# GpSimd loads the FFN weights, ScalarE takes signs, copies and seven normalizations, VectorE merges statistics and shares the last low parts

## What is computed

```
x = x + dwconv7x7(layernorm_c(x), w_sym)
t = tokens(x)                              # (16, 1024, 192)
h = layernorm(t) @ sign(W1 - mean_g(W1)).T + b1      # 768 hidden, weights in 5 groups of rows
h = gelu(clip(h * 128 / (max|h| + 1e-5)))  # the maximum over a group of 3 images
y = h @ sign(W2 - mean_g(W2)).T + b2
out = t + clip(y * 128 / (max|y| + 1e-5))  # again a group maximum
```

## Time and profile before

| | us |
|---|---|
| median of 3 runs (lowest, highest) | 699.06 (697.81, 699.81) |
| the profiled execution | 697.41 |
| its span, first to last instruction | 695.6 |
| busy: TensorE, VectorE, ScalarE, GpSimd | 510.0, 455.9, 383.2, 217.0 |
| mean granted TensorE clock | 0.884 of full |

### The profile page before, as it was taken

One profiled execution on the slowest core, in us unless ns is written; L12 is line 12 of the kernel. 1 busy time (PEld: TensorE's weight loads), 2 busy tenths in 40 slices (PEclk: granted clock), 3 DMA queues, 4 the chain that ended last, 5 costly groups with the idle time before them and its releaser, 6 DMA issues.

```text
span 695.6 us, 9929 instructions
## 1 busy us (share of the span) xinstructions
PE 510.0 (73%) x3552; PEld 356.9 (51%) x3552; DVE 455.9 (66%) x1106; ACT 383.2 (55%) x612; POOL 217.0 (31%) x195
## 2 busy tenths in 40 slices
PE   4254179995299874656778979997999799778763
PEld 4254179995299873323334535554555455345342
DVE  8988922221068587599888686788878878644432
ACT  3799710000000301443799989997999799787400
POOL 4000100000000000000056756475656557678900
PEclk9778589998599995788999999999999999989865
DMA  8997136654254519900011000131222333142444
GB/s 221 304 333 186 53 82 172 167 167 138 87 149 130 152 49 362 340 0 0 13 55 47 24 24 0 47 91 64 74 69 91 96 109 92 47 135 73 135 138 155
DMA packets 55270, 81.29 MB, mean 117 GB/s; under 512 B 7161, under 2 KB 38905, under 8 KB 55222
## 3 DMA queue, kind: packets, MB, share of 16 engines
q1 hardware_dynamic: 40416, 68.93, 32.2%
q10 hardware_dynamic: 14806, 11.73, 5.7%
HBM read 53.12 MB, written 27.53 MB: 116 GB/s over the span
## 4 chain that ended last, share of the span: by engine, by line
PE 37%; ACT 22%; DVE 17%; DMA 10%; issue 5%; POOL 3%; ACTq 3%; SPq 2%; POOLq 0%; DVEq 0%
PE bank L873 15%; ACT arena L486 9%; ACT arena L480 6%; PE bank L947 5%; DMA arena<-kz_d 5%; DMA arena<-x 4%; DVE am L745 4%; POOL arena L373 3%; DVE arena L726 2%; PE bank L922 2%; DVE arena L672 2%; PE bank L924 2%; ACT arena L504 2%; PE bank L923 2%; ACT arena L466 2%
## 5 line engine op out<-in xcount | busy, mean ns | idle before, releaser
L373 POOL TENSOR_TENSOR arena<-arena 128x512 f16<-128x512 f32 x180 | 204.2, 1174 | 297.3 <-DVE arena L741 297.3
L873 PE MATMUL bank<-arena 128*128 128x112 f32 (+1 forms) x1152 | 137.1, 283 | 45.1 <-DMA arena<-kz_d 29.2
L873 PEld LDWEIGHTS bank<-arena 128*128 128x128 f32 x1152 | 135.5, 199 | 46.7 <-issue 27.0
L480 ACT ACTIVATE arena<-bank,b1s 128x512 f32<-128x512 f32 x180 | 126.1, 703 | 57.4 <-PE bank L924 57.0
L947 PE MATMUL bank<-arena 128*128 128x512 f16 x360 | 110.0, 402 | 30.4 <-ACT arena L504 19.0
L486 ACT ACTIVATE arena<-arena,gm 128x1024 f32<-128x1024 f32 x90 | 102.6, 1161 | 5.6 <-DVE gm L767 5.6
L656 DVE TENSOR_TENSOR arena<-bank,arena 128x512 f32<-128x512 f32 x48 | 33.2, 691 | 103.7 <-PE bank L873 103.6
L745 DVE TENSOR_REDUCE am<-arena 128x1 f32<-128x3072 f32 x30 | 100.3, 3343 | 0.0
L922 PE MATMUL bank<-arena 128*128 128x512 f16 x180 | 71.2, 396 | 33.9 <-DVE arena L734 14.5
L429 ACT ACTIVATE arena<-arena,wmean 51x576 f16<-51x576 f32 (+1 forms) x10 | 7.6, 840 | 136.1 <-DVE wmean L625 136.1
L947 PEld LDWEIGHTS bank<-arena 128*128 128x128 f16 x360 | 34.0, 101 | 79.3 <-issue 35.2
(11 more groups left out here) (115 smaller groups left out, 655.2 us busy)
## 6 DMA issues: line engine op xcount, KB each, us to landing
arena<-park_d SPq DMA_DIRECT2D x44, 384.0 KB, 3.4
arena<-kz_d SPq DMA_DIRECT2D x100, 112.0 KB, 2.8
arena<-kz_d ACTq DMA_DIRECT2D x92, 112.0 KB, 3.2
park_d<-arena SPq DMA_DIRECT2D x6, 1536.0 KB, 13.9
arena<-x SPq DMA_DIRECT2D x8, 1024.0 KB, 8.6
out<-arena SPq DMA_DIRECT2D x32, 256.0 KB, 2.0
kz_d<-arena SPq DMA_DIRECT2D x8, 672.0 KB, 11.3
arena<-x SPq DMA_DIRECT2D x16, 256.0 KB, 9.8
```

The lines of the kernel that those rows point to most:

```text
L373: last = pool.tensor_tensor(out=low_half(u, m, m + 1), in0=yslot(u)[:, 2 * m:2 * m + 2, :], in1=hib(u, m, m + 1), op=ALU.subtract)
L480: act.activation(yslot(s)[:, 2 * m:2 * m + 2, :], m1p[c % 2][:, :].rearrange("p (h n) -> p h n", h=2), ACT.Identity, bias=b1s[:, m:m + 1], ...
L873: last = t.matmul(ps[:, :, lo:hi], WB[BUFS[g]][:, 1 - db, c, :], xn[:, :, lo + db:hi + db], start=(db == 0), stop=(db == -1))
```

## The change

- The ten loads of W1 and W2 are issued by GpSimd, after group 24; it also clears the ends of the transposed weights. Its first memset is cut into six.
- ScalarE makes one sign operation after each band load from group 38 on, and copies the transposed signs out of PSUM (four for W1 behind the band loads, six for W2 first thing in step -2). The sums move to groups 28 to 32, the means' matmul to after group 33.
- Front: for the last unit ScalarE copies before it takes the root of the unit before, and VectorE takes the factors of the unit before in the middle of the last statistics.
- The statistics of channels 0 to 127 are ready by group 45 and are merged for all images at once in group 46; the merging per batch has nine operations and one; four batches instead of five.
- ScalarE does `normal` for half images 1 to 7. In step -2 it takes the root before it copies image 16.
- High parts: ScalarE tiles 0 and 1, VectorE 2 to 5; for half images from 23 on ScalarE 0 to 3 and VectorE 4 and 5. Low parts from half image 23 on: GpSimd tiles 0 to 2, VectorE 3 to 5. TensorE takes the products of the tiles in the order 2 to 5, 0, 1 (from 23 on 3 to 5, 0 to 2).
- `result` of channels 0 to 127 is taken at the end of the step of its products, up to step 29.
- The x of half images 25 to 29 is loaded at step 30 into five buffers; 25 and 26 are transposed in step 31 and 27 in step 39, into PSUM banks that are free by then; 28 and 29 after the final sums of 24 and 25. ScalarE's queue stores their upper channels.

```diff
-BATCH = ((0, 2), (2, 6), (6, 10), (10, 12), (12, 15))
-BSTEP = (-2, -1, 0, 1, 2)
-FREED = {3: 2, 4: 3, 5: 3, 6: 4, 7: 5, 8: 5}
+BATCH = ((0, 2), (2, 6), (6, 10), (10, 15))
+BSTEP = (-2, -1, 0, 1)
...
+ANORM = range(1, 8)
...
+HA, HL, LP = 2, 4, 3
+LAST = FT - LAGH
+ORDER = {False: (*range(HA, MT), *range(HA)), True: (*range(LP, MT), *range(LP))}
...
+def ha(u):
+    return HL if u >= LAST else HA
...
+early = list(range(FT - GT + 1, FT))
+at = XB + WW + WTN
+XE = [*XL, *(view(at + i * RB * C, RB * C).rearrange("p (n c) -> p n c", n=RB) for i in range(2))]
+turned = {v: pair for v, pair in zip(early, ((bank[0], bank[1]), (tA, tB), (m2a, m2b), (xA, xB), (bank[0], bank[1])))}
...
+        if s == FT:
+            sp.wait_ge(tnv, FT)
+            for i, h in enumerate(early):
+                if i == 3:
+                    sp.wait_ge(trQ, FT)
+                sp.dma_start(XE[i].rearrange("p n c -> p (n c)"), park_d[h - 2 * KEPT]).then_inc(ld_g[i], 16)
...
+    for i in range(6):
+        last = pool.memset(view(R + i * WW // 3, WW // 3), 0.0)
+    last.then_inc(blank, 1)
...
+    pool.wait_ge(conv, ROOM[FOURTH] + 1)
+    for q in range(GROUPS):
+        pool.dma_start(w1w[0:RP1, q, :], w1[q * 3 * RP1:(q + 1) * 3 * RP1, :]
+                       .rearrange("(p r) c -> p (r c)", r=3)).then_inc(ld_w, 16)
+        pool.dma_start(w2w[0:RP2, q, :], w2[q * RP2:(q + 1) * RP2, :]).then_inc(ld_w, 16)
...
+    for u in range(LAST):
+        pool.wait_ge(hiV, u + 1)
+        low(u, HA, MT)
+        pool.wait_ge(hiA, u + 1)
+        low(u, 0, HA)
+    for u in range(LAST, FT):
+        pool.wait_ge(hiA, u + 1)
+        low(u, 0, LP)
...
+        if k == PAIRS - 1:
+            bring(k)
         if k:
             deviation(k - 1)
-        if k < PAIRS:
+        if k < PAIRS - 1:
...
+        if g >= 38:
             act.wait_ge(prep_mean, 2)
-            for q in range(GROUPS):
-                sign(w1s[q][0:RP1], w1w[0:RP1, q, :].rearrange("p (r c) -> p r c", r=3), wmean[0:RP1, q:q + 1])
-        if g == 40:
-            for q in range(GROUPS):
-                sign(w2s[q][0:RP2], w2w[0:RP2, q, :].rearrange("p (m f) -> p m f", m=MT),
-                     wmean[0:RP2, GROUPS + q:GROUPS + q + 1])
+            signs(g - 38)
...
+    act.wait_ge(prep_t, 1)
+    for dst, src, ch in ((W1A, t1a, slice(0, P)), (W1Q, t1b, slice(0, P)), (W1M, t1a, slice(0, C1)),
+                         (W1M, t1b, slice(C1, P))):
+        o = dst[ch, 0:n].rearrange("p (g q r) -> p g r q", g=GROUPS, r=3)
+        i = src[ch, :].rearrange("p (g r q) -> p g r q", g=GROUPS, r=3)[:, :, :, 0:RP1]
+        act.activation(o, i, ACT.Copy).then_inc(prep_done, 1)
...
+    def second_weights():
+        act.wait_ge(prep_t, 2)
+        for m in range(MT):
+            act.activation(W2T[:, m, 0:GROUPS * RP2].rearrange("p (g q) -> p g q", g=GROUPS), t2[m], ACT.Copy) \
+                .then_inc(prep_done, 1)
+    def normal(h):
+        act.wait_ge(nm, PAIRS + taken(h // 2))
+        if h >= 2:
+            act.wait_ge(trQ, h - 1)
+        for jj in range(RB):
+            n = RB * h + jj
+            last = act.activation(TN[:, h % 2, jj, :], X1[:, n, :], ACT.Identity, bias=SM[:, n:n + 1], scale=VR[:, n:n + 1])
+        last.then_inc(tnv, 1)
...
+            second_weights()
+            deviation2(0)
             x_alone(0)
             x_alone(1)
-        if s == -2:
-            deviation2(0)
...
-        if 0 <= w < FT:
+        if s > FT and 0 <= w < FT:
             result(w, 0)
...
+            if m < 2 and 0 <= k < FT and 2 * m < ha(k):
+                high(k, 2 * m, 2 * m + 2)
             if m == 0 and 0 <= w < FT:
                 result(w, 1)
+            if m == MT - 1 and 0 <= s - LAG2 and s < FT:
+                result(s - LAG2, 0)
...
+        if s + 2 in ANORM:
+            normal(s + 2)
+    for u in early:
+        act.wait_ge(fin, u + 1)
+        store_upper(act, u, u % Y2R, st_o[u % Y2R])
...
+            if k == PAIRS - 1 and j == NB // 2:
+                factors1(k - 1)
...
+        if 0 < k < PAIRS - 1:
+            factors1(k - 1)
             normal1(k - 1)
         if k < PAIRS:
             stats1(k)
+        if k == PAIRS - 1:
+            normal1(k - 1)
...
+    def lower_whole():
+        dve.wait_ge(bnA, NN)
+        v.tensor_tensor(out=SA[:, :, 0], in0=SA[:, :, 1], in1=SA[:, :, 4], op=ALU.add).then_inc(mixA, 1)
+        v.tensor_tensor(out=SA[:, :, 3], in0=SA[:, :, 1], in1=SA[:, :, 4], op=ALU.subtract).then_inc(mixA, 1)
...
-        if 32 <= g < 48:
-            lower_statistics((g - 32) * per, (g - 31) * per)
-        if 27 <= g < 27 + GROUPS:
-            weight_sums(g - 27)
-        if g == 37:
+        if 32 <= g < 32 + PARTS:
+            lower_statistics((g - 32) * NN // PARTS, (g - 31) * NN // PARTS)
+        if 28 <= g < 28 + GROUPS:
+            weight_sums(g - 28)
+        if g == 35:
             weight_means()
-        if g == 45:
-            weight_copies(0)
+        if g == 32 + PARTS:
+            lower_whole()
...
+        v.scalar_tensor_tensor(out=SM[:, cols], in0=SM[:, cols], scalar=-1.0 / 6.0, in1=VR[:, cols], op0=ALU.mult,
+                               op1=ALU.mult).then_inc(nm, 1)
...
+        v.tensor_copy(hib(u, ha(u), MT), yslot(u)[:, 2 * ha(u):2 * MT, :]).then_inc(hiV, 1)
+        if u >= LAST:
+            dve.wait_ge(hiV, u + 1)
+            low(u, HL, MT)
+            dve.wait_ge(hiA, u + 1)
+            low(u, LP, HL)
+    def low(u, m0, m1):
+        v.tensor_tensor(out=low_half(u, m0, m1), in0=yslot(u)[:, 2 * m0:2 * m1, :], in1=hib(u, m0, m1),
+                        op=ALU.subtract).then_inc(lo2v, 1)
...
-        if -1 <= s <= 5:
-            normal(s + 2)
...
+        order = ORDER[u >= LAST]
+        m = order[i]
+        if i == 0:
+            if u < LAST:
+                pe.wait_ge(lo2, lows(u) - 1)
             if u >= 1:
                 pe.wait_ge(ev2, 2 * u - 1)
+        if u >= LAST and m >= LP:
+            pe.wait_ge(lo2v, 2 * (u - LAST) + (1 if m >= HL else 2))
+        if m == 0:
+            pe.wait_ge(lo2, lows(u))
...
+        if s == FT + 1:
+            pe.wait_ge(ev1, MT * FT)
+            pe.wait_ge(ld_g[0], 16)
+            x_back(early[0], XE[0], xpl)
+            pe.wait_ge(tlo, 2 * FT)
+            pe.wait_ge(ld_g[1], 16)
+            x_back(early[1], XE[1], xpl)
+        if s == FT + LAGF - GT:
+            pe.wait_ge(ev2, 2 * FT)
+            pe.wait_ge(ld_g[2], 16)
+            x_back(early[2], XE[2], xpl)
+    for i in (3, 4):
+        pe.wait_ge(fin, early[i] - 3)
+        pe.wait_ge(ld_g[i], 16)
+        x_back(early[i], XE[i], xpl)
```

156 lines of the change are left out of this document (72 added, 84 removed).

## The result

The changed kernel takes 638.7 us at the median (635.5 to 640.3), the kernel before 698.6 (697.8 to 699.8): a ratio of 0.9135, 95% interval 0.9092 to 0.9178. It is faster by 60 us, where 83 were forecast, and 2.7 us outside the range. The profiled execution has a span of 638.1 us against 695.6: 57.5 us.

| stage, from event to event | before, us | after, us | gain | forecast |
|---|---|---|---|---|
| start to first convolution matmul | 88.8 | 87.3 | 1.5 | 2 |
| to the eviction of group 23 | 71.4 | 73.2 | -1.8 | 0 |
| to the eviction of group 28 | 37.8 | 17.8 | 20.0 | 23 |
| to the end of the last eviction | 63.2 | 54.5 | 8.7 | 3 + 4.5 |
| to the GELU table load | 86.1 | 73.5 | 12.6 | 16 |

The account below looks back on a forecast made before the run. No engine was taken to own the span, so each stage was priced at its last-ending wait. Terms summing to 83 us took the profiled 697.41 to 614.4, or 616 us as a median 1.65 higher; range 602 to 636.

Parts of the forecast that it names:

- Last results: Last six half images: GpSimd keeps three low parts instead of six, ScalarE becomes slowest at 5.95 us each; 11 us gained.
- Steady steps: FFN steps to about 603 us: early result removes TensorE's 0.64 us wait, leaving its own 9.85 per step; 10 us gained.
- Weight loads: Convolution near group 26: loads off ScalarE's queue end the 21.83 us TensorE pause for bands; 23 us gained.
- no TensorE wait over 3 us: Sign to look for: between groups 24 and 30 TensorE never waits over 3 us for band weights.
- Lead-in: Last eviction to GELU table load: fewer VectorE operations and normalizations moved to ScalarE bring it from +86.1 to +70; 16 us.
- Signs, means and end of the convolution: Later convolution: spread signs remove a 3.92 us pause, 3 us; W1 copies moved to ScalarE end it earlier, 4.5 us.
- Front: Load and first normalization: split memset and earlier ScalarE copies bring the first convolution matmul forward; 2 us gained.
- Final sums: End of kernel: inputs loaded and partly transposed ahead, so six sums of 1.15 us run in a row; 13.5 us gained.
- 1: Rival: weight loads still stop the bands in the convolution, the pause stays; 637 us, chance 0.13.
- 4: Rival: slower, every VectorE operation of a steady step excludes GpSimd, steps take 15.8 us; 751 us, chance 0.02.
- 2: Rival: another engine takes the limit in lead-in and steps, lead-in 11, steps 2 instead of 26; 629 us, chance 0.15.
- 3: Rival: last part gains half, VectorE and GpSimd exclude each other, TensorE at 1.2 GHz; 623 us, chance 0.08.

Follow-up runs that it names:

- tail_sum_first: Changed kernel with VectorE's output sum ahead of the high and low parts in the steps after the last hidden matmul: 627.7 us, ratio 0.901.
- last_24: Changed kernel with VectorE's steps reordered, the maxima row one product later, and low-part sharing from half image 24 instead of 23: 613.7 us, ratio 0.880.
- weights_pairs: Against last_24: GpSimd's weight loads issued four, four and two after groups 24, 25, 26; sums, their matmul and means one group later: 616.0 us, ratio 0.881.

## Why the prediction was right or wrong

- *Last results (11 us): this step failed.* "The slowest is then ScalarE: ... 5.95 per half image." ScalarE's work was priced right, and GpSimd's nearly (3.9 us for three parts, not 3.5), but the sum took each engine's own work for the period and never followed the order in which they wait. With the low parts on VectorE, ahead of the output sum, they came into the ring of sum, turned input, upper matmuls and high copy, and the ring took 7.33 us. The part from result 21 on lost 3.6 us instead of gaining some 10 (the 11 of this term less the 0.9 charged to the last border). Moving only the sum gives 5.94 (shown). The 2.1 us for the late first gelu were foreseen; switching the sharing off gave back 1.4 to 2.7 at that border (shown), and starting it one half image later 2.8.
- *Steady steps (10 us): right in the plain step, mis-sized at the border.* 9.80 us came as worked out, and undoing the early result costs some 6 us (shown). The four borders were charged 0.9 us each for VectorE's cast and the gelu; measured against before they cost 2.1, 2.8, 1.2 and 4.4 in this execution (2.1 of the last were foreseen, in the last part's term). The text had no wait of TensorE for the maxima and no clock after it. A faster TensorE comes earlier to the same maximum: at the second and third border its wait grew from 1.22 to 2.71 us, and in part of the borders half the clock followed. From result 0 to 21 the gain was 6.0 us here and 6.0 to 9.5 in six others of the same steady steps.
- *Weight loads (23 us): mechanism right, size off.* Putting the loads back on ScalarE's queue brings the pause back (shown). Whether it is their standing ahead of the band loads or their few engines (share 0.19) isn't separated, for from GpSimd's queue they lost both. Left is a wait of 2.58 us here and 2.4 to 5.7 in all in other executions (the sign "no TensorE wait over 3 us" held here and failed in four of them), because the ten loads take 5.5 us of all engines, not 3.5, within 14 us in which the convolution leaves 36%, that is 5.0. The 1.4 us allowed for it should have been 3 to 9 (31.0 to 37.0 us for groups 23 to 33, against 28.0 with half the loads). The Trainium skill, "DMA: Bandwidth & Descriptors", section "Why a DMA increments its semaphore by 16 and not by 1", has loads from GpSimd spread over all sixteen engines or over a few that move on from load to load. The trace agrees with a spread (share 1.03 instead of 0.19) and the share doesn't tell which of the two it was. The 24 us that the prediction took from it was further off than the 23, since a spread says nothing about the amount.
- *Lead-in (16 us): right in the way, somewhat short in size.* The table load stood 73.5 us behind the last eviction in this execution (12.6 gained), 70.1 to 72.9 in twelve others; forecast 70, with 11 as the low bound of the gain.
- *Signs, means and end of the convolution (7.5 us):* 8.7. The new wait at the matmul of the sums was forecast at 1.4 and measured 1.35. *Front (2):* 1.5. *Final sums (13.5):* 13.0; six sums in 6.3 us, forecast 6.9.
- *The early convolution, -1.8 us, not in the text.* Other executions of the same code up to there took 71.3 to 74.7 us, the one profile of before 71.4; whether the change has a part in it stays open.
- *Rivals.* 1 and 4 fell. 2 names the region rightly, lead-in and steps, but its 629 assumed a lead-in of 11, and what limited the borders was a wait, not an engine's load. 3 pointed at the last part, but its reason wasn't the one: the exclusion of VectorE and GpSimd was there but hidden (below), and the final sums gained their 13.0.
- *The bounds.* Added up, the low terms give 650 and the high ones 601 us, not the 648 and 598 of the text; nothing else hangs on them.

What stays open is when the clock falls: it fell at some borders and held at others with the same wait (2.71 us twice in tail_sum_first; 3.62 us in last_24, where it held, and in weights_pairs, where it fell), so the runs give no rule. Open is also how much of a long border is clock and how much is order.

## What to carry to other kernels

When work moves from the busiest engine to an idler one, look at what stands behind it on the new engine and who waits for that; add up the ring through all engines, not each engine's load. When a step gets shorter, every wait for a chain that didn't get shorter (a group maximum) grows by as much: put independent products ahead of that point before taking the gain as won. Bulk loads beside a stream that uses two thirds of the DMA engines cost by their amount: moving them off the stream's queue took away the long pause (22 us here), not that.
